# A graph kernel of four layers: TensorE adds up the weighed rows, edge counts are laid out with destinations innermost, and ScalarE copies and turns them one pair later

## The chip, the cores and the metric

The kernel runs on one core of one Trainium2 chip. The metric is the device time of one execution in microseconds (us). The core has TensorE (matmuls, into PSUM), VectorE, ScalarE, GpSimd and SyncE, each with its own in-order queue of instructions. In the profile they are PE (PEld is the loading of the stationary operand), DVE, ACT, POOL and SP; a q behind a name is the queue itself (register, branch and DMA-issuing instructions).

## The reference

A graph of 3125 nodes and 103125 edges, features of 128 floats. Four layers stand one behind the other, each `x = x + layer(relu(layernorm(x)))`. The change touches what two of them and a preparation compute.

```python
# layer 0: three hops of attention over 64 kinds of relation
for _ in range(3):
    h = agg[head]; t = agg[tail]; rel = edge_emb[edge_type]
    att = jnp.sum((h @ q_w) * jnp.tanh(rel * t @ k_w), axis=1)
    w = softmax of att over the edges of each head
    agg = segment_sum(w[:, None] * rel * t, head) / count      # then normalised, added to out
# layer 1: three graph attention layers with 4 heads, layer 2: two graph convolutions
# layer 3: composed attention over 474 kinds
comp = ent_emb[src] + rel_emb[rel_id]
norm = softmax of jnp.sum(comp * ent_emb[dst], axis=-1) over the edges of each dst
out = jnp.tanh(segment_sum(comp * norm[:, None], dst) @ neigh_w)
```

Layers 1 and 2 do not walk over edges. They use a dense matrix with the number of edges between each source and each destination (3200 x 3200), and its logarithm, which a preparation makes once.

## The kernel before

The nodes are sorted by degree and cut into NB = 25 blocks of P = 128, one node on each partition. The edges of a block stand in *bodies*: a body holds S = 8 neighbours for each of the 128 nodes, and a block takes as many bodies as its largest degree needs. All blocks together have 116 bodies. A *half* of a body is H = 4 neighbours.

Every engine runs its own program for a stage, in loops whose counts are read from the plan; semaphores tie the engines together. There is no scheduler: the order on each engine is the order in which the code is written. `stand` is a semaphore wait followed by a count of it, so a wait there shows as "issue" in the trace.

**`count_pairs`** (the preparation) takes the blocks two at a time, 13 *pairs* in all, the last with one block. For a pair VectorE splits the neighbour numbers into a high and a low part (`split`), TensorE turns them, ScalarE copies them out (`splitT`). VectorE makes the one-hot tiles: `hi_hot` of the high part and, in 8 chunks of 16 destinations, `lo_hot` of the low part, two chunks alternating. For a chunk TensorE does 32 matmuls (16 destinations, 2 blocks, contraction over 64 neighbours) into `chunk_ps`, and VectorE adds the chunk into `counts`, which GpSimd has cleared. A pair whose nodes have over 64 neighbours takes more steps of this kind; in this execution each pair takes one. Then TensorE turns the 25 x 2 squares of `counts` (`turn_counts`), ScalarE copies them out in 14 pieces and sends them to memory, and takes the logarithm of `counts` into `logs`; VectorE scales the logs (`tell`), and a DMA that ScalarE issues sends them. `counts`, `logs` and `turned_sb` exist twice.

**`attention_over_relations`** (the relation layers, three hops). GpSimd gathers the rows of a body, eight indirect DMAs (`PairStream.gather_all`); `land` holds two bodies, and `rows_used` gives a half free again. Per body VectorE makes a one-hot of the kinds (`kinds`), multiplies rows and relation vectors (`messages`, one half at the beginning and one at the end of its body), adds the weighed rows of the body before (`add_body`, which calls `Softmax.add`), takes eight dot products (`product`) and does the running softmax (`scores`). TensorE turns the one-hot (`turn_kinds`), turns and projects each half of the messages (`rights`) and makes the relation vectors (`relations`). ScalarE copies between them, takes tanh and the exponentials, and weighs each of the eight rows by its probability (`weigh`, into `weighed`). At the end of a block VectorE divides and stores (`finish_block`).

**`composed_attention`** (the composed layer, one pass over the 116 bodies). Per body TensorE spreads the kinds over all partitions (`widen_kinds`, into `line_ps`), ScalarE copies that line out (`move_line`), VectorE compares it with the kinds (`hots`), and TensorE makes the relation vectors out of 96 bf16 matmuls (`relations`, into `rel_ps`), which VectorE adds to the gathered rows (`compose`). Dot products, softmax, weighing and adding up are as above. VectorE works on body n, composes n+1 and makes one-hots for n+2; TensorE widens n+3.

The rows are added up in `Softmax.add` on VectorE: the 8 x 128 weighed elements of a partition are reduced over the eight (L981), and the running total is scaled (L978) and added to (L984).

## Time and profile before

| | us |
|---|---|
| median of 3 runs (10826.94 to 10835.59) | 10832.68 |
| the profiled execution | 10814.64 |
| its span | 10812.8 |
| pair counts, about 1495 to 2200 of the span | 705 |
| relation layers, three hops, 2310 to 6030 | 3720 |
| graph attention and graph convolution, between | about 3270 |
| composed layer, 9380 to 10760 | 1380 |

The profiled execution's time is the one that its trace adds up to; it lies 18.0 us below the median of the runs. A group of instructions in the profile is named by line, engine, operation, and output and inputs; numbers behind `x` are counts. "Idle before" is time in which the engine stood still ahead of such an instruction, with what ended it behind the arrow.

### The profile page before, as it was taken

The numbers are of one execution on the slowest core, as the hardware profiler recorded it, in microseconds if no ns is written. First come the engines' busy times: TensorE is split into PE (matmuls) and PEld (weight loads), VectorE is DVE, ScalarE is ACT, GpSimd is POOL, SyncE is SP. The second block draws the span as 40 slices with busy tenths as digits, with TensorE's granted clock in tenths as the row PEclk, the third lists the DMA queues.
The fourth block names the chain that finished last, engine by engine and source line by source line (L and its number), as shares of the span: only waits on it lengthen the run. The fifth ranks groups of instructions, "written<-read, shape, count | busy, mean of one in ns | idle before, by whom it ended". The sixth has DMA issues, their size and how long they took to land. (4 is left out here: it accounts for less than half of the span.)

```text
span 10812.8 us, 222859 instructions
## 1 busy us (share of the span) xinstructions
PE 6848.0 (63%) x64938; PEld 5402.2 (50%) x64939; DVE 8324.0 (77%) x22674; ACT 6175.0 (57%) x11492; POOL 6853.0 (63%) x5770
## 2 busy tenths in 40 slices
PE   3984952236666566656666477777777768466665
PEld 2973952235554455545555344444544534366665
DVE  9779778857777677767777699899989970477776
ACT  4224222236666566646666499899979960155554
POOL 0777731057776777767777488878868610466665
PEclk8555556568887788877888799999999989777777
DMA  0111114322222222222222211111111126322212
GB/s 22 57 37 28 60 33 143 129 61 53 53 53 48 49 53 53 53 46 52 53 53 53 38 43 49 50 38 49 46 41 49 49 72 250 74 48 47 46 45 44
DMA packets 415976, 627.20 MB, mean 58 GB/s; under 512 B 273479, under 2 KB 327073, under 8 KB 392169
## 3 DMA queue, kind: packets, MB, share of 16 engines
q0 software_dynamic: 192432, 385.10, 16.3%
q1 hardware_dynamic: 156048, 155.60, 4.6%
q10 hardware_dynamic: 67401, 85.32, 2.2%
q8 instruction: 50, 0.82, 0.0%
q14 instruction: 45, 0.37, 0.0%
HBM read 525.80 MB, written 101.39 MB: 58 GB/s over the span
## 5 line engine op out<-in xcount | busy, mean ns | idle before, releaser
L895 POOL DMA_INDIRECT l_land<-table,l_words x3744 | 3580.1, 956 | 1338.0 <-issue 1153.7
L1674 POOL DMA_INDIRECT ell<-gat_stage_pay,gat_stage_at x816 | 1899.5, 2328 | 248.7 <-issue 248.7
L1365 PE MATMUL left_product_ps<-k_w,messageT 128*128 128x128 f32 x5616 | 1036.5, 341 | 531.6 <-ACT messageT L1400 531.6
L1365 PEld LDWEIGHTS left_product_ps<-k_w,messageT 128*128 128x128 f32 x5616 | 873.4, 237 | 736.4 <-ACT messageT L1400 736.4
L1723 PE MATMUL gat_ps<-gat_probT,h 128*32 128x128 f32 x15000 | 823.7, 292 | 436.2 <-ACT gat_probT L1774 290.3
L2234 PE MATMUL rel_ps<-relation_parts,hot 128*128 128x128 bf16 x11328 | 821.0, 247 | 414.8 <-DVE hot L2333 414.6
L244 POOL DMA_INDIRECT ell<-pay,position x816 | 841.6, 1031 | 290.8 <-issue 281.6
L1359 PE MATMUL left_turned_ps<-ident,message 128*128 128x128 f32 x2808 | 557.7, 333 | 728.2 <-DVE message L1491 728.2
L2234 PEld LDWEIGHTS rel_ps<-relation_parts,hot 128*128 128x128 bf16 x11328 | 800.7, 113 | 436.2 <-DVE hot L2333 436.2
L1416 ACT ACTIVATE weighed<-kept,l_prob 128x128 f32 x2784 | 889.1, 391 | 59.1 <-ACT l_prob L961 59.1
L1714 PE MATMUL gat_ps<-ident,gat_logit 128*128 128x128 f32 x5625 | 824.5, 285 | 44.4 <-ACT gat_logit L1767 43.3
L1851 DVE SCALAR_TENSOR_TENSOR gat_logit<-gat_source_row,gat_own,gat_logit 128x3200 f32<-128x3200 f32 x225 | 797.6, 3545 | 68.3 <-DMA gat_logs<-logs,perm 58.4
L1855 DVE CUSTOM_DVE_ANT_0 gat_logit<-gat_logit,gat_logs 128x3200 f32<-128x3200 f32 x225 | 785.7, 3492 | 27.2 <-issue 2.9
L1359 PEld LDWEIGHTS left_turned_ps<-ident,message 128*128 128x128 f32 x2808 | 384.7, 172 | 830.7 <-DVE message L1491 828.5
L295 PE MATMUL looked_ps<-count,loT_wide 128*128 (+1 forms) x3264 | 755.6, 384 | 48.5 <-issue 45.3
L295 PEld LDWEIGHTS looked_ps<-count,loT_wide 128*128 128x128 f32 x3264 | 744.6, 333 | 57.3 <-issue 54.7
L1351 PE MATMUL rel_ps<-relation_parts,hotT 128*128 128x256 bf16 x4248 | 771.2, 333 | 2.0 <-ACT hotT L1395 2.0
L1412 ACT ACTIVATE right<-left_product_ps 128x512 f32<-128x512 f32 x702 | 418.1, 596 | 602.3 <-DVE l_score L1552 343.3
L1723 PEld LDWEIGHTS gat_ps<-gat_probT,h 128*32 128x32 f32 x15000 | 354.0, 110 | 770.0 <-ACT gat_probT L1774 513.7
L1714 PEld LDWEIGHTS gat_ps<-ident,gat_logit 128*128 128x128 f32 x5625 | 620.7, 142 | 230.7 <-issue 230.7
L1767 ACT ACTIVATE gat_logit<-gat_logit,gat_peak 128x3200 f32<-128x3200 f32 x225 | 667.4, 2966 | 114.9 <-DVE gat_peak L1855 103.3
L981 DVE TENSOR_REDUCE part<-weighed 128x128 f32<-128x1024 f32 x348 | 667.3, 1917 | 27.1
(332 smaller groups left out, 16142.2 us busy)
## 6 DMA issues: line engine op xcount, KB each, us to landing
gcn_edges<-counts SPq DMA_DIRECT2D x50, 1600.0 KB, 7.4
l_land<-table,l_words POOLq DMA_INDIRECT x3744
rows<-low_dram SPq DMA_DIRECT2D x34, 1536.0 KB
counts<-pair_turned_sb ACTq DMA_DIRECT2D x12, 3200.0 KB, 9.4
logs<-pair_logs ACTq DMA_DIRECT2D x12, 3200.0 KB, 18.2
ell<-pay,position POOLq DMA_INDIRECT x816
ell<-gat_stage_pay,gat_stage_at POOLq DMA_INDIRECT x816
l_words<-ell SPq DMA_DIRECT2D x476, 8.0 KB
```

Source lines behind the costliest of these rows:

```text
L244: pool.indirect_dma_start(c.ells[0][:, :], bass.IndirectOffsetOnAxis(ap=position[:, 0, t:t + 1], axis=0), pay[:, t, :], None).then_inc(pla ...
L295: pe.matmul(looked_ps[r % HALVES][:, j, :], loT_wide[:, r % CAST, j, :], count[:, bass.ds(tile + j, 1), :].rearrange("p a n -> p (a n)"), ...
L895: pool.indirect_dma_start(self.land[:, p, s, :], None, table[:, :], bass.IndirectOffsetOnAxis(ap=self.words[:, p, s, 0:1], axis=0)).then_i ...
L1359: mm = pe.transpose(messageT_ps[:, k * H + j, :], message[:, k * H + j, :], c.ident[:, :])
L1365: mm = pe.matmul(right_ps[:, k * H + j, :], messageT[:, k, j, :], k_w[:, :], start=True, stop=True)
L1416: last = nc.scalar.activation(weighed[:, s, :], kept[:, bass.ds(n % 2, 1), s, :].rearrange("p a d -> p (a d)"), ACT.Copy, scale=soft.prob[ ...
L1674: pool.indirect_dma_start(c.ells[1][:, :], bass.IndirectOffsetOnAxis(ap=stage_at[n % 2][:, t:t + 1], axis=0), stage_pay[n % 2][:, t, :], N ...
L1714: mm = pe.transpose(ps[:, q % 4, r * P:(r + 1) * P], logit[t][:, j * P:(j + 1) * P], c.ident[:, :])
L1723: mm = pe.matmul(ps[C * r:C * (r + 1), 4 + t % 2, 0:P], xs[:, 4 * q + r, t * C:(t + 1) * C], probT[q % 4][:, r, :], start=(q == 0), stop=( ...
L1851: V.scalar_tensor_tensor(out=logit[t][:, :], in0=source_row[:, t, :], scalar=own[:, bass.ds(i, 1), t:t + 1].rearrange("p a b -> p (a b)"), ...
L1855: V.tensor_tensor_reduce(logit[t][:, :], logit[t][:, :], logs[k][:, :], op0=ALU.add, op1=ALU.min, scale=-1.0, scalar=3.0e38, accum_out=pea ...
L2234: mm = pe.matmul(rel_ps[:, k * H + s, :], hot[:, k, g, s, :], parts[:, g, t, :], start=(g == 0 and t == 0), stop=(g == PARTS - 1 and t == 2))
```

## The change

Three edits.

In both edge layers (relation layers and composed layer) the eight weighed rows are added by TensorE: eight f32 matmuls with the identity as stationary operand that accumulate in a PSUM tile `sum_ps` (`add_up`). VectorE takes the finished sum in one instruction with the scaling of the total (`Softmax.add_sum`). Two semaphores, `sum_ready` and `sum_used`, pass the tile to and fro.

In `count_pairs` the one-hot tiles and their comparison constants `hi_iota`, `lo_iota` are laid out with the neighbours' or destinations' axis innermost, so that both inputs of the comparison have an innermost step of one element; TensorE then reads columns that lie 128 and 16 elements apart. The first step of a pair is no longer added to cleared counts but copied into them by ScalarE; the clears by GpSimd are gone.

Also in `count_pairs`, the turning, the sending and the logarithm of a pair (`turn_counts` on TensorE, `finish` on ScalarE) stand behind the next pair's counting, and VectorE's `tell` one pair later too.

```diff
+    def add_sum(self, v, total, weighed_sum, sum_ready, n, sum_used):
+        V = self.nc.vector
+        v.wait_ge(self.prob_ready, n)
+        V.tensor_copy(self.top_now[:, :], self.top_new[:, :])
+        V.tensor_reduce(self.part[:, :], self.prob[:, :, :].rearrange("p s h -> p h s"), AX.X, ALU.add)
+        v.drain()
+        V.scalar_tensor_tensor(out=self.denom[:, :], in0=self.denom[:, :], scalar=self.keep[:, 0:1], in1=self.part[:, :],
+                               op0=ALU.mult, op1=ALU.add)
+        v.wait_ge(sum_ready, n)
+        V.scalar_tensor_tensor(out=total[:, :], in0=total[:, :], scalar=self.keep[:, 0:1], in1=weighed_sum[:, :],
+                               op0=ALU.mult, op1=ALU.add).then_inc(sum_used, 1)
...
-        hi_hot = sb("pair_hi_hot", [P, P, NB], BF16)
-        lo_hot = sb("pair_lo_hot", [P, 2, CHUNK, P], BF16)
+        hi_hot = sb("pair_hi_hot", [P, NB, P], BF16)
+        lo_hot = sb("pair_lo_hot", [P, 2, P, CHUNK], BF16)
+        hi_iota, lo_iota = sb("pair_hi_iota", [P, NB, P], BF16), sb("pair_lo_iota", [P, P, CHUNK], BF16)
...
-            @block.gpsimd
-            def _(pool):
-                for p in range(PAIRS):
-                    if p >= 2:
-                        pool.wait_ge(turned, (p - 1) * 2 * TURNS)
-                        pool.wait_ge(logged, p - 1)
-                    nc.gpsimd.memset(counts[p % 2][:, :, :, :], 0.0).then_inc(cleared, 1)
...
-                    pe.wait_ge(summed, p + 1)
+                    many, first = steps(pe, p)
+                    pe.wait_ge(kept, (first + many) * CHUNKS_OF + 2)
...
-                                    mm = pe.matmul(chunk_ps[u % 2][:, b, j * NB:(j + 1) * NB], lo_hot[half, u % 2, j, :],
-                                                   hi_hot[half, u * CHUNK + j, :], start=True, stop=True)
+                                    mm = pe.matmul(chunk_ps[u % 2][:, b, j * NB:(j + 1) * NB], lo_hot[half, u % 2, :, j],
+                                                   hi_hot[half, :, u * CHUNK + j], start=True, stop=True)
...
-                    turn_counts(p, k, parts)
-                pair(0, 0)
+                pair(0)
                 with pe.Fori(0, PAIRS // 2 - 1) as two:
                     for k in range(2):
-                        pair(two * 2 + (k + 1), 1 - k)
-                pair(PAIRS - 2, 1)
-                pair(PAIRS - 1, 0, 1)
+                        pair(two * 2 + (k + 1))
+                        turn_counts(two * 2 + k, k, 2)
+                pair(PAIRS - 2)
+                turn_counts(PAIRS - 3, 0, 2)
+                pair(PAIRS - 1)
+                turn_counts(PAIRS - 2, 1, 2)
+                turn_counts(PAIRS - 1, 0, 1)
...
-                def pair(p, k, earlier, parts=2):
+                def pair(p, k):
                     many, first = steps(act, p)
                     with act.Fori(0, many) as g:
                         n = act.snap(first + g)
                         act.wait_ge(split_turned, n + 1)
                         nc.scalar.copy(splitT[:, :, :], split_ps[:, :, :]).then_inc(split_moved, 1)
+                        with act.If(g < 1):
+                            for u in range(CHUNKS_OF):
+                                act.wait_ge(counted, n * CHUNKS_OF + (u + 1))
+                                nc.scalar.copy(counts[k][:, :, :, u * CHUNK:(u + 1) * CHUNK].rearrange("p h b j -> p b j h"),
+                                               chunk_ps[u % 2][:, :, 0:CHUNK * NB]
+                                               .rearrange("p b (j h) -> p b j h", h=NB)).then_inc(kept, 1)
+                def finish(p, k, earlier, parts=2):
                     act.wait_ge(counts_out[k], earlier * 16 + 16)
...
-                pair(0, 0, 0)
+                pair(0, 0)
+                pair(1, 1)
+                finish(0, 0, 0)
                 with act.Fori(0, PAIRS // 2 - 1) as two:
                     for k in range(2):
-                        pair(two * 2 + (k + 1), 1 - k, two + k)
+                        pair(two * 2 + (k + 2), k)
+                        finish(two * 2 + (k + 1), 1 - k, two + k)
                         tell(two * 2 + k, k)
-                pair(PAIRS - 2, 1, PAIRS // 2 - 1)
+                pair(PAIRS - 1, 0)
+                finish(PAIRS - 2, 1, PAIRS // 2 - 1)
                 tell(PAIRS - 3, 0)
-                pair(PAIRS - 1, 0, PAIRS // 2, 1)
+                finish(PAIRS - 1, 0, PAIRS // 2, 1)
                 tell(PAIRS - 2, 1)
...
-                for k in range(2):
-                    V.memset(logs[k][:, :, :, :], 0.0)
+                V.tensor_copy(hi_iota[:, :, :], spread(c.iota_rb[:, 0:NB], [P, NB, P], 2))
+                V.tensor_copy(lo_iota[:, :, :], spread(c.iota_rb[:, :], [P, P, CHUNK], 2))
...
-                        V.tensor_tensor(hi_hot[:, :, :], spread(c.iota_rb[:, 0:NB], [P, P, NB], 1),
-                                        spread(splitT[:, 1, :], [P, P, NB], 2), ALU.is_equal)
+                        V.tensor_tensor(hi_hot[:, :, :], hi_iota[:, :, :], spread(splitT[:, 1, :], [P, NB, P], 1),
+                                        ALU.is_equal)
                         def hot(u):
-                            V.tensor_tensor(lo_hot[:, u % 2, :, :], spread(c.iota_rb[:, :], [P, CHUNK, P], 1),
-                                            spread(splitT[:, 0, u * CHUNK:(u + 1) * CHUNK], [P, CHUNK, P], 2),
+                            V.tensor_tensor(lo_hot[:, u % 2, :, :], lo_iota[:, :, :],
+                                            spread(splitT[:, 0, u * CHUNK:(u + 1) * CHUNK], [P, P, CHUNK], 1),
                                             ALU.is_equal).then_inc(hot_ready, 1)
                         hot(0)
                         hot(1)
-                        for u in range(CHUNKS_OF):
-                            v.wait_ge(counted, n * CHUNKS_OF + (u + 1))
-                            total = counts[k][:, :, :, u * CHUNK:(u + 1) * CHUNK].rearrange("p h b j -> p b j h")
-                            V.tensor_tensor(total, chunk_ps[u % 2][:, :, 0:CHUNK * NB]
-                                            .rearrange("p b (j h) -> p b j h", h=NB), total, ALU.add).then_inc(kept, 1)
-                            if u + 2 < CHUNKS_OF:
-                                hot(u + 2)
-                        v.drain()
-                    v.sem_inc(summed, 1)
+                        with v.If(g < 1):
+                            for u in range(2, CHUNKS_OF):
+                                v.wait_ge(counted, n * CHUNKS_OF + (u - 1))
+                                hot(u)
+                        with v.If(g > 0):
+                            for u in range(CHUNKS_OF):
+                                v.wait_ge(counted, n * CHUNKS_OF + (u + 1))
+                                total = counts[k][:, :, :, u * CHUNK:(u + 1) * CHUNK].rearrange("p h b j -> p b j h")
+                                V.tensor_tensor(total, chunk_ps[u % 2][:, :, 0:CHUNK * NB]
+                                                .rearrange("p b (j h) -> p b j h", h=NB), total, ALU.add).then_inc(kept, 1)
+                                if u + 2 < CHUNKS_OF:
+                                    hot(u + 2)
...
+                pair(1, 1)
+                with v.Fori(0, PAIRS // 2 - 1) as two:
                     for k in range(2):
-                        pair(two * 2 + (k + 1), 1 - k)
+                        pair(two * 2 + (k + 2), k)
                         tell(two * 2 + k, k)
-                tell(PAIRS - 1, 0)
+                pair(PAIRS - 1, 0)
+                for p in range(PAIRS - 3, PAIRS):
+                    tell(p, p % 2)
...
+                def add_up(w):
+                    pe.wait_ge(sum_used, w + 1)
+                    for k in range(HALVES):
+                        pe.wait_ge(weighed_ready[k], w + 1)
+                    for s in range(S):
+                        mm = pe.matmul(sum_ps[:, :], c.ident[:, :], weighed[:, s, :], start=(s == 0), stop=(s == S - 1))
+                    mm.then_inc(sum_ready, 1)
...
                             rights(n + i + 1, k)
                             relations(m + i + 2, k)
+                        add_up(hop * all_bodies + i)
...
-                    for k in range(HALVES):
-                        v.wait_ge(weighed_ready[k], n)
-                    soft.add(v, weighed, total, part, D)
+                    soft.add_sum(v, total, sum_ps, sum_ready, n, sum_used)
...
+                def add_up(n):
...
                     widen_kinds(i + 3)
+                    add_up(i)
                     for k in range(HALVES):
                         relations(i + 2, k)
...
-                        for k in range(HALVES):
-                            v.wait_ge(weighed_ready[k], n + 1)
-                        soft.add(v, weighed, total, part, D)
+                        soft.add_sum(v, total, sum_ps, sum_ready, n + 1, sum_used)
```

What the program order is at the two places on TensorE and at the one on ScalarE on which the most hangs.

TensorE in the composed layer, the loop over bodies of `composed_attention`, before (`line_ps` is the widening, `rel_ps` the relation vectors):

```order
L2243 UNCONDITIONAL_BRANCH
L2243 ISA
L2223 MATMUL line_ps<-ident_b,kind_b 128x128 x8
L2229 REGISTER_ALU
L2234 MATMUL rel_ps<-relation_parts,hot 128x128 x96
L2243 REGISTER_ALU
L2243 COMPARE_AND_BRANCH
```

The same loop in the change:

```order
L2292 ISA
L2263 MATMUL line_ps<-ident_b,kind_b 128x128 x8
L2280 REGISTER_ALU
L2284 MATMUL l_sum_ps<-weighed,ident 128x128 x8
L2269 REGISTER_ALU
L2274 MATMUL rel_ps<-relation_parts,hot 128x128 x96
L2292 REGISTER_ALU
```

The sum of body i now stands between the widening for body i+3 and the relation vectors of body i+2.

TensorE in the relation layers, the loop over bodies of `attention_over_relations`, in the change (`left_turned_ps` holds the turned messages, `left_product_ps` their projection, each once for a half; before, the same rows stand without the two of the sum):

```order
L1369 MATMUL hotT_ps<-ident_b,hot 128x128 x4
L1386 ISA
L1388 MATMUL left_turned_ps<-ident,message 128x128 x4
L1390 REGISTER_ALU
L1394 MATMUL left_product_ps<-k_w,messageT 128x128 x4
L1376 REGISTER_ALU
L1380 MATMUL rel_ps<-relation_parts,hotT 128x256 x6
L1388 MATMUL left_turned_ps<-ident,message 128x128 x4
L1394 MATMUL left_product_ps<-k_w,messageT 128x128 x4
L1380 MATMUL rel_ps<-relation_parts,hotT 128x256 x6
L1400 ISA
L1404 MATMUL l_sum_ps<-weighed,ident 128x128 x8
```

The sum of body i stands last in its round, behind everything that this round makes for the bodies i+1 and i+2.

ScalarE in `count_pairs`, from the split copy of a pair to the first turned copies, before:

```order
L1131 CAST pair_splitT<-pair_split_ps 128x256
L1128 REGISTER_ALU
L1128 COMPARE_AND_BRANCH
L1132 ISA
L1137 ISA
L1138 COPY pair_turned_sb<-pair_turned_ps 128x512
```

And in the change, the end of the eight chunk copies and what follows them:

```order
L1145 COPY pair_counts<-pair_chunk_ps 128x2x16x25
L1142 UNCONDITIONAL_BRANCH
L1138 REGISTER_ALU
L1138 COMPARE_AND_BRANCH
L1150 ISA
L1155 ISA
L1156 COPY pair_turned_sb<-pair_turned_ps 128x512
```

Eight copies of chunks have come between, and the turned copies behind them are those of the pair before.

## Rows read from the trace of the kernel before

**Rows 1.** By stretch: length, busy PE, PEld, DVE, ACT, POOL; granted clock, DMA.

```profile
1495.00:2200.00 705.00, 181.60 (x3979) 139.98 (x3979) 570.31 (x351) 164.04 (x202) 70.57 (x13) 0.59 0.34 119
2310.00:6030.00 3720.00, 2319.43 (x14222) 1854.47 (x14222) 2778.91 (x12201) 2297.82 (x5958) 2722.26 (x2854) 0.80 0.26 51
9380.00:10760.00 1380.00, 884.10 (x12219) 855.09 (x12217) 1080.12 (x4990) 696.85 (x1630) 894.82 (x930) 0.79 0.24 46
```

**Rows 2.** Who waited for whom, 2320 to 6010: us in total, times, longest.

```profile
POOL l_land L895 <- issue: 866.7, 2777, 5.8
...
DVE hot L1482 <- SPq L864: 394.3, 282, 7.6
```

**Rows 3.** Groups of instructions on GpSimd, 2320 to 6010.

```profile
L895 POOL DMA_INDIRECT l_land<-table,l_words x2796 | 2667.4, 954 | 873.0 <-issue 866.7 <-SPq L864 6.4
```

**Rows 4.** Instructions that read weighed rows: ns min/median/max, first and last start.

```profile
L981 DVE TENSOR_REDUCE l_sum<-weighed x116: 1901/1918/1949, 9397.0 to 10744.8; 128x128 f32<-128x1024 f32 x116
```

**Rows 5.** Timeline of one pair in the counts: start, length in us, instruction.

```profile
1817.84 0.59 ACT L1138 COPY pair_turned_sb<-pair_turned_ps 128x512 f32<-128x512 f32 x1 [35.64 <-PE pair_turned_ps L1088]
...
1827.55 5.63 ACT L1146 ACTIVATE pair_logs<-pair_counts,pair_few 128x6400 f32<-128x6400 f32 x1 [0.60 <-ACT pair_turned_sb L1138]
...
1839.22 0.61 PE L1107 MATMUL pair_chunk_ps<-pair_hi_hot,pair_lo_hot 64*128 64x25 bf16 x32 [10.76 <-DVE pair_lo_hot L1224]
```

**Rows 6.** Instructions of line 1220: ns min/median/max, first and last start.

```profile
L1220 DVE TENSOR_TENSOR pair_hi_hot<-iota_rb,pair_splitT x13: 3491/3493/3493, 1524.0 to 2140.5; 128x3200 bf16<-128x3200 bf16 x13
```

**Rows 7.** Groups of instructions by shape on VectorE, whole span and counts stage.

```profile
L1224 DVE TENSOR_TENSOR pair_lo_hot<-iota_rb,pair_splitT 128x2048 bf16<-128x2048 bf16 x104 | 236.7, 2287 | 0.0
...
L1233 DVE TENSOR_TENSOR pair_counts<-pair_chunk_ps,pair_counts 128x800 f32<-128x800 f32 x104 | 177.0, 1716 | 0.0
...
L1243 DVE SCALAR_TENSOR_TENSOR pair_logs<-pair_logs 128x6400 f32<-128x6400 f32 x13 | 88.7, 6825 | 6.7 <-issue 4.2 <-ACT pair_logs L1146 2.4
...
L675 DVE TENSOR_REDUCE col<-x 128x25 f32<-128x3200 f32 x4 | 14.0, 3488 | 94.9 <-PEq L2422 91.2 <-PEq L599 3.7
...
L1196 DVE MEMSET pair_logs<- 128x6400 f32 x2 | 10.8, 5392 | 3.0 <-issue 3.0
...
L692 DVE TENSOR_SCALAR h<-h 128x3200 f32<-128x3200 f32 x4 | 7.3, 1826 | 0.3
```

**Rows 8.** Timeline of one body in the relation layers.

```profile
4003.61 0.69 DVE L1491 TENSOR_TENSOR message<-l_land,rel_ps 128x512 f32<-128x512 f32 x1
...
4005.93 1.16 PE L1365 MATMUL left_product_ps<-k_w,messageT 128*128 128x128 f32 x8 [0.92 <-ACT messageT L1400]
...
4006.93 0.82 PE L1351 MATMUL rel_ps<-relation_parts,hotT 128*128 128x256 bf16 x6
...
4010.07 0.29 DVE L1552 CUSTOM_DVE_ANT_0 product<-right,left_now 128x128 f32<-128x128 f32 x1
...
4013.00 0.69 DVE L1491 TENSOR_TENSOR message<-l_land,rel_ps 128x512 f32<-128x512 f32 x1
```

**Rows 9.** Timeline of a body, composed layer; relations of a later body.

```profile
10014.51 0.62 PE L2223 MATMUL line_ps<-ident_b,kind_b 128*128 128x128 bf16 x8 [1.94 <-DVE kind_b L2324]
...
10015.38 1.28 ACT L2270 ACT_TABLE_LOAD   x1 [3.94 <-PE line_ps L2223]
...
10018.06 2.45 ACT L2282 ACTIVATE weighed<-kept,l_prob 128x128 f32 x8 [0.17 <-ACT l_prob L961]
...
10019.37 6.91 PE L2234 MATMUL rel_ps<-relation_parts,hot 128*128 128x128 bf16 x96 [4.23 <-DVE hot L2333]
...
10065.08 5.53 PE L2234 MATMUL rel_ps<-relation_parts,hot 128*128 128x128 bf16 x96 [2.04 <-DVE hot L2333]
```

**Rows 10.** Groups of instructions on VectorE, 2320 to 6010, last step of a block.

```profile
L1510 DVE TENSOR_SCALAR res<-total,scale 128x128 f32 x72 | 21.1, 293 | 12.2 <-issue 12.2
```

**Rows 11.** Busy time by stretch as in group 1, during the relations at 10019.37.

```profile
10019.30:10021.00 1.70, 1.63 (x16) 1.64 (x17) 1.70 (x7) 1.70 (x7) 1.40 (x2) 0.50 0.12 28
...
10024.00:10026.30 2.30, 2.27 (x41) 2.10 (x38) 0.76 (x4) 0.00 (x0) 1.82 (x2) 1.00 0.21 57
```

22 lines of the change are left out of this document (16 added, 6 removed).

## The prediction, made before the kernel ran

> **What bounds the kernel now.** I first cut the execution into stages with the windows view. The change touches three of them [rows 1]: the pair counts (705 us), the relation layers with their three hops (3720 us), and the composed layer at the end (1380 us). In each of them VectorE has the largest busy sum, or nearly so, and that sum alone would say: relieve VectorE. The waits say something else.
>
> In the relation layers GpSimd's gathers wait for nothing but their own issue (866.7 us over 2777 gathers, 0.31 us each), while VectorE waits 394.3 us for SyncE's word that rows have landed [rows 2]. A gather takes 0.954 us and with its idle time 3540.4 / 2796 = 1.27 us [rows 3]; eight make a body, and without the long waits 8 x (0.954 + 0.30) = 10.05 us. So GpSimd paces this stage, and VectorE work taken away there buys nothing. What can do harm is a chain that becomes longer than 10.05 us.
>
> In the composed layer the 116 bodies start (10744.8 - 9397.0) / 115 = 11.72 us apart [rows 4], above the 10.05 of the same gathers: here VectorE's chain does set the pace, so a shorter one could win up to 1.67 us a body, 192 us in all.
>
> In the pair counts ScalarE sits idle for 35.64 us before its turned copies [rows 5], and VectorE does everything one after the other: the thirteen first one-hot tiles start (2140.5 - 1524.0) / 12 = 51.4 us apart [rows 6].
>
> **Pair counts: what the change is worth.** A chunk costs VectorE a low one-hot of 2287 ns and an addition of 1716 ns [rows 7]; eight chunks are 32 us of the 51.4. Every pair has one step, so afterwards VectorE adds nothing: ScalarE copies each chunk. The one-hots get an innermost step of one on both 2-byte inputs. No row shows such a two-input operation. Above, its price is today's 2287 ns for 2048 elements; below, the kernel's 3200-element one-input operation that passes two elements a cycle takes 1826 ns [rows 7], 0.57 ns an element, or 1.17 us for 2048. I take the lower one, 1.83 for the high and 1.2 for each low tile, since all operands then lie side by side. The Trainium skill, page "Vector Engine (DVE) Microarchitecture Reference", section 5.1, has a rule for it: two inputs and an output of 2-byte type, all at innermost step one, run two elements a cycle, also where a row is read again and again. By that rule this stage comes to -249 us, by today's row to -120; no row here shows such an operation.
>
> ScalarE's copy is 800 elements from PSUM, written with a jump of 256 elements between neighbours. Below, it costs what a copy of 512 does (0.59 us, [rows 5]) carried to 800, 0.83 us. Above, it costs what VectorE's addition into the same places does, 1.72. VectorE's sum over rows that it reads by jumps takes 1918 ns for 1024 elements [rows 4], 1.87 ns each, against 3488 / 3200 = 1.09 side by side [rows 7]: a jump costs 0.78. 800 x (0.83 + 0.78) + 160 ns gives 1.45 us, which I take. The same page, section 5.2, puts a destination that jumps at every element at 1.71 ns an element for VectorE. By it a copy would take about 1.5 us and the stage would save 4 us less; no row here has ScalarE writing with jumps.
> TensorE's 32 small matmuls of a chunk take 0.61 us [rows 5] and now read both operands with gaps; I allow 1.2 us, hidden beside the copy. Nothing shows it; at over 1.5 us it would be the chunk's pace.
>
> ScalarE now has a pair's whole chain: split copy 0.35; wait for the high tile, the first low tile and the first matmuls, 1.8 + 1.2 + 0.6 and 0.4 of handovers, 4.0; eight copies 11.7; turned copies of the pair before, 1817.84 to 1827.55 with their DMA, 9.7, by [rows 5]; logarithm 5.63 [rows 5]; register loads and gaps, about 2. Sum 33.4 us in place of 51.4. VectorE's own (1.8, 8 x 1.2, 6.8 for the scaling of the logs [rows 7], some 3 for the small steps) is 21 and hidden. Eleven intervals save 11 x 18 = 198 us. The interval between the first two pairs holds no turning: 17.5 in place of 51.4, 34 more. The end gets a second turning and logarithm behind the last chunk (+16) but a shorter last pair (one-hots and additions 3.5 + 8 x 3.9 = 35 before; 3.6 + 11.7 = 15.5 after; -20). At the start VectorE's two clears of the logs, 5.4 us each [rows 7], become two copies of 3200 and 2048 elements, some 4 us in all, and the clears of the counts on GpSimd go, up to 6 more: -13 taken. Together **-249 us**, bounds -120 (VectorE at its old rate, copies hidden) and -310 (copies of 0.83).
>
> **Relation layers.** VectorE loses its sum over eight rows (1.9 us of a body) and waits for TensorE's instead. Read one body [rows 8]. The second message ends at 4004.30 = T. ScalarE turns it over behind its first four weighings; TensorE's products start at 4005.93, its relations end at 4007.75, T + 3.45. Today VectorE starts its dot products at 4010.07 and ends the next second message at 4013.69: a loop of 9.39 us. The new sum stands behind those relations on TensorE's queue. Its price: four f32 products take 1.16 us [rows 8], eight 2.3; bounds 0.62 (eight bf16 matmuls, [rows 9]) and twice 2.3 at half clock. So it ends at T + 5.75, VectorE adds it by T + 6.1, and dot products, scores and message (4010.07 to 4013.69, 3.62) end at T + 9.75. Closing a block lies on this loop too: its last step takes 0.29 us and 0.17 of idle before it [rows 10], three shorter steps and two clears bring it to about 1.4 us, every 348 / 75 = 4.64 bodies, 0.3 a body: **10.05 us, exactly GpSimd's pace**. At equality every delay shows; I put **+70 us** (0.2 a body) on 348 bodies. Nothing is won, since GpSimd's pace stays. The bounds are 0 and, if TensorE falls to its lower clock once a block and 4.1 us of its work in the loop doubles, 4.1 / 4.64 x 348 = +310.
>
> **Composed layer.** Here the place of the new sum on TensorE decides. The program order per body is: widen the kinds of body i+3, sum body i, relations of body i+2, 96 matmuls. ScalarE's order is: copy out the widened line, exponentials of body i, weigh. So the widening waits behind the relations of the body before, the weighing behind the widening, the sum behind the weighing, and the relations behind the sum. All of it is one ring. Its pieces [rows 9]: widening to table load 10014.51 to 10015.38, 0.87; table load and line copy, to the weighing's start at 10018.06, 2.68; weighing 2.45; handover 0.05; sum 2.3; relations 5.53 less 0.1 of overlap, 5.4. Ring: **13.75 us**. Today the ring does not exist: relations start when the one-hots are there, and the weighing of body i delays none of them.
> In the new ring TensorE idles 5.4 us from the widening's end to the sum. In the trace, idle of 4.2 us ahead of the relations has them begin at a granted clock of 0.50 and go on at 1.00 [rows 11], and they take 6.91 us in place of 5.53 [rows 9], 1.4 more. The sum and the relations will pay that: 15.15 us. (15.15 - 11.72) x 115 = **+394 us**. At full clock it would be +233; with 1.4 us more, +555. VectorE's saved 1.92 us [rows 4] only lengthens its wait for the sum. The Trainium skill, page "TensorE: Matmul & The Clock Gate", part "Why this matters for your kernels", advises against idle gaps between bursts of matmuls, since the clock falls in them. It speaks against this ring: by it the body takes 15.15 us, without it 13.75, and the two durations of the relations agree with it.
>
> **Sum.** -249 + 70 + 394 = +215 us. The profiled execution took 10814.6 us (span 10812.8 and 1.8 around it), the median of the three runs is 18 us above it. 10832.7 + 215 = 11048, so **11050 us**. About 0.2% is what a measurement of this kernel can tell from no change.
>
> **The rivals.**
> 1. The composed layer really follows VectorE (*faster*). VectorE's chain without the reduction is at most 11.72 - 1.92 = 9.80 us, so GpSimd's 10.05 would decide: -192 us, relation layers 0, counts -249: 10390 us. For it speaks that today's trace shows VectorE as this stage's pace; against it the program order above. It decides itself at one point: whether the widening starts before the relations of the body before have ended. Chance 0.07.
> 2. A cheap sum (*faster or equal*). Eight matmuls with one and the same stationary operand at about 1.2 us, full clock, copies of 0.83: ring 12.65 (+107), relation layers 0, counts -310, in all about -200: 10630. With only part of it the result is near zero. Chance 0.13.
> 3. The relation layers leave GpSimd's pace, as TensorE drops its clock once a block: +310 in place of +70: 11290. For it: TensorE's work now lies in a loop without slack. Against it: TensorE idles less there than today. Chance 0.12.
> 4. The one-hots stay at one element a cycle, or the gapped operands slow the chunk to over 2 us: counts -120, 11180. Chance 0.08.
> My forecast has 0.60.
>
> **How the numbers follow.** Below 10811 lie rival 1 and most of 2: faster 0.18, same 0.04, slower 0.78. The forecast's own range is 10930 to 11190 (counts by 60, composed layer by 90 either way); taking in rivals 3 and 4 and the upper part of 2, 10790 to 11300.
>
> **What the new profile would show.** Counts: low one-hots of 1.2 us, ScalarE copies of 1.45, first tiles 33 us apart. Relation layers: sums 2.3 us, bodies at 10.0 to 10.4, granted clock nearer 1. Composed layer: bodies 15 us apart, TensorE idle 5 us ahead of the sum and released by the weighing, ScalarE waiting for the widened line, GpSimd waiting for the rows to be used. The prediction is wrong if the bodies there stand 10 to 12 us apart, or if the relation layers grow by more than 200 us.

## The result, and the profile of the changed kernel

The changed kernel takes **11241 us** (median of four runs, 11228 to 11256), the kernel before beside it 10830: a ratio of 1.038, 95% interval [1.0366, 1.0392], slower by 411 us. 11050 was forecast. 11241 lies above the forecast's own range (10930 to 11190) and within the wide one (10790 to 11300), which reaches so far up only because rival 3 (11290) was taken in. The sign and the largest part were right; one term, the relation layers, was far too small.

First the stages, in the windows view of the changed kernel (length of the stretch, busy time of PE, PEld, DVE, ACT and POOL, granted clock, DMA):

```profile
1478.00:1953.00 475.00, 256.42 (x4047) 217.16 (x4046) 264.99 (x272) 326.89 (x309) 0.00 (x0) 0.61 0.51 177
2065.00:6045.00 3980.00, 2856.38 (x19782) 2450.95 (x19782) 2058.97 (x11155) 2287.33 (x5957) 2765.64 (x2851) 0.85 0.25 48
9400.00:11202.00 1802.00, 1156.23 (x14075) 1133.73 (x14073) 849.44 (x4642) 696.49 (x1630) 897.63 (x929) 0.83 0.19 35
```

They answer to [rows 1]. VectorE lost work in all three, 305, 720 and 231 us, and yet two of the three are longer. To measure the edge stages closely, take the first and last start of one instruction that every body has, the update of the running total; before and after (nanoseconds least/median/most, then first and last start):

```profile
L978 DVE TENSOR_TENSOR total<-total,l_keep x348: 278/284/341, 2332.8 to 6008.1; 128x128 f32<-128x128 f32 x174
```

```profile
L973 DVE SCALAR_TENSOR_TENSOR total<-total,l_keep,l_sum_ps x348: 337/347/349, 2084.5 to 6024.5; 128x128 f32<-128x128 f32 x174
...
L973 DVE SCALAR_TENSOR_TENSOR l_total<-l_total,l_keep,l_sum_ps x116: 346/347/350, 9419.0 to 11185.3; 128x128 f32<-128x128 f32 x116
```

The first update comes 2332.8 - 2084.5 = 248 us earlier: the counts. The relation layers grow from 3675.3 to 3940.0, **+265 us**. The composed layer grows from 1347.8 [rows 4] to 1766.3, **+418.5**. Together +435; some 6 us more lie between the stages, and the spans differ by 11254.1 - 10812.8 = 441. The medians differ by 411 only: the profiled execution of before lies 18 us below the median of its runs, the profiled one of the changed kernel 15 above. So the stage figures, read from one execution each, hold some 30 us of scatter in all.

**Pair counts.** The groups of the stage (busy us and mean ns, then idle time before and its releaser):

```profile
L1145 ACT COPY pair_counts<-pair_chunk_ps 128x800 f32<-128x800 f32 x104 | 161.3, 1667 | 56.3 <-PE pair_chunk_ps L1114 56.2
L1114 PE MATMUL pair_chunk_ps<-pair_hi_hot,pair_lo_hot 64*128 64x25 bf16 x3328 | 125.8, 221 | 124.8 <-DVE pair_lo_hot L1245 94.0 <-ACT pair_counts L1145 30.4 <-issue 0.2
L1245 DVE TENSOR_TENSOR pair_lo_hot<-pair_lo_iota,pair_splitT 128x2048 bf16<-128x2048 bf16 x104 | 125.1, 1223 | 24.3 <-PE pair_chunk_ps L1114 24.3
...
L1241 DVE TENSOR_TENSOR pair_hi_hot<-pair_hi_iota,pair_splitT 128x3200 bf16<-128x3200 bf16 x13 | 23.7, 1825 | 136.9 <-ACT pair_splitT L1141 136.9
```

The tile that took 2287 ns [rows 7] takes 1223, the high one 1825 instead of 3493 [rows 6]. ScalarE copies a chunk in 1667 ns, and VectorE waits 136.9 us in all for ScalarE's split copy. ScalarE sets the pace, as forecast.

**Relation layers.** Their waits (us in total, times, longest):

```profile
DVE total L973 <- PE l_sum_ps L1404: 1261.2, 330, 5.7
...
POOL l_land L895 <- issue: 824.3, 2608, 5.7
...
POOL l_land L895 <- DVE message L1531: 242.3, 182, 2.5
...
DVE hot L1522 <- SPq L864: 136.6, 34, 8.2
```

Read against [rows 2] the direction has turned. Before, VectorE waited for rows (394.3 us) and GpSimd for nothing. Now GpSimd waits 242.3 us for VectorE's messages to free its buffer, and VectorE stands still 3.8 us in nearly every body (330 of 348) until TensorE's sum is done. Two bodies one behind the other:

```profile
3001.39 0.69 DVE L1531 TENSOR_TENSOR message<-l_land,rel_ps 128x512 f32<-128x512 f32 x1
...
3005.28 1.95 PE L1404 MATMUL l_sum_ps<-weighed,ident 128*128 128x128 f32 x16
...
3007.26 0.35 DVE L973 SCALAR_TENSOR_TENSOR total<-total,l_keep,l_sum_ps 128x128 f32<-128x128 f32 x1 [2.88 <-PE l_sum_ps L1404]
...
3010.58 0.69 DVE L1531 TENSOR_TENSOR message<-l_land,rel_ps 128x512 f32<-128x512 f32 x1
...
3012.81 1.57 PE L1394 MATMUL left_product_ps<-k_w,messageT 128*128 128x128 f32 x8 [0.83 <-ACT messageT L1439]
...
3014.17 1.49 PE L1380 MATMUL rel_ps<-relation_parts,hotT 128*128 128x256 bf16 x6
...
3015.45 2.60 PE L1404 MATMUL l_sum_ps<-weighed,ident 128*128 128x128 f32 x16
...
3018.09 0.35 DVE L973 SCALAR_TENSOR_TENSOR total<-total,l_keep,l_sum_ps 128x128 f32<-128x128 f32 x1 [2.99 <-PE l_sum_ps L1404]
...
3019.42 0.29 DVE L1548 TENSOR_SCALAR res<-total,scale 128x128 f32 x1 [0.17 <-issue]
```

The first, from message to message, takes 9.19 us. In the second the same three pieces of TensorE's work cost 1.57, 1.49 and 2.60 us, not 1.16, 0.82 and 1.95, and a block closes at its end. The windows view gives the clock of the two sums and of what lies ahead of the second (columns as above):

```profile
3005.40:3007.20 1.80, 1.80 (x20) 1.79 (x19) 0.00 (x0) 0.36 (x1) 1.29 (x2) 1.00 0.15 36
3012.90:3014.30 1.40, 1.40 (x9) 1.34 (x10) 1.04 (x2) 1.40 (x5) 0.94 (x1) 0.68 0.17 47
3014.30:3015.60 1.30, 1.30 (x8) 0.99 (x7) 0.73 (x5) 0.71 (x2) 0.95 (x1) 0.50 0.19 50
3015.60:3018.00 2.40, 2.40 (x19) 2.39 (x18) 0.00 (x0) 0.00 (x0) 1.89 (x2) 0.75 0.21 55
```

**Composed layer.** One turn of the ring in the timeline of the changed kernel:

```profile
10008.32 0.61 PE L2263 MATMUL line_ps<-ident_b,kind_b 128*128 128x128 bf16 x8
...
10009.18 1.28 ACT L2320 ACT_TABLE_LOAD   x1 [9.75 <-PE line_ps L2263]
...
10011.86 2.44 ACT L2332 ACTIVATE weighed<-kept,l_prob 128x128 f32 x8 [0.17 <-ACT l_prob L961]
...
10014.44 3.50 PE L2284 MATMUL l_sum_ps<-weighed,ident 128*128 128x128 f32 x16 [5.52 <-ACT weighed L2332]
...
10017.78 5.52 PE L2274 MATMUL rel_ps<-relation_parts,hot 128*128 128x128 bf16 x96
...
10023.14 0.61 PE L2263 MATMUL line_ps<-ident_b,kind_b 128*128 128x128 bf16 x8
```

Each link releases the next; this turn takes 14.82 us and the mean over 116 bodies is 1766.3 / 115 = 15.36. The sum takes 3.50 us, at a granted clock of 0.53:

```profile
10014.60:10017.70 3.10, 3.10 (x16) 3.10 (x17) 0.00 (x0) 0.72 (x2) 2.31 (x3) 0.53 0.16 45
```

One turn is an example. The waits of the whole stage show the same links in all 116 bodies, and the groups give TensorE's mean (busy us and ns of one record, 16 records a sum and 96 a body's relations):

```profile
ACT L2320 <- PE line_ps L2263: 1061.2, 116, 9.7
...
PE l_sum_ps L2284 <- ACT weighed L2332: 640.1, 116, 5.5
```

```profile
L2274 PE MATMUL rel_ps<-relation_parts,hot 128*128 128x128 bf16 x11223 | 697.3, 227 | 0.0
...
L2284 PE MATMUL l_sum_ps<-weighed,ident 128*128 128x128 f32 x1856 | 420.6, 419 | 640.1 <-ACT weighed L2332 640.1
```

A sum takes 420.6 / 116 = 3.63 us in the mean, so nearly every one of them pays for the lower clock; and the relations never wait for their one-hots, only for the sum ahead of them.

### The profile page after: what moved, and what is told of

It reads as the page before. It is cut to its first block and busy times, and to the rows that moved or that the text cites. A ratio compares the mean times of both kernels' runs of the same rounds, so it can differ in the third digit from the quotient of the medians.

```text
span 11254.1 us, 236447 instructions
## 1 busy us (share of the span) xinstructions
PE 7727.1 (69%) x72362; PEld 6349.4 (56%) x72363; DVE 7061.9 (63%) x21178; ACT 6326.1 (56%) x11596; POOL 6837.0 (61%) x5757
## 5 line engine op out<-in xcount | busy, mean ns | idle before, releaser
L895 POOL DMA_INDIRECT l_land<-table,l_words x3744 | 3629.8, 969 | 1939.6 <-issue 1089.0
L1394 PE MATMUL left_product_ps<-k_w,messageT 128*128 128x128 f32 x5616 | 965.5, 324 | 533.5 <-ACT messageT L1439 532.6
L1394 PEld LDWEIGHTS left_product_ps<-k_w,messageT 128*128 128x128 f32 x5616 | 808.7, 222 | 711.8 <-ACT messageT L1439 710.7
L973 DVE SCALAR_TENSOR_TENSOR total<-total,l_keep,l_sum_ps 128x128 f32<-128x128 f32 x348 | 120.7, 347 | 1261.2 <-PE l_sum_ps L1404 1261.2
L2284 PE MATMUL l_sum_ps<-weighed,ident 128*128 128x128 f32 x1856 | 420.6, 419 | 640.1 <-ACT weighed L2332 640.1
L1404 PEld LDWEIGHTS l_sum_ps<-weighed,ident 128*128 128x128 f32 x5568 | 816.9, 233 | 15.1
L1404 PE MATMUL l_sum_ps<-weighed,ident 128*128 128x128 f32 x5568 | 823.5, 311 | 0.0
L1434 ACT COPY hotT<-hotT_ps 128x512 bf16<-128x512 bf16 x354 | 207.5, 586 | 1042.1 <-PE hotT_ps L1369 1042.1
L1388 PE MATMUL left_turned_ps<-ident,message 128*128 128x128 f32 x2808 | 474.2, 294 | 459.1 <-DVE message L1531 458.9
L2284 PEld LDWEIGHTS l_sum_ps<-weighed,ident 128*128 128x128 f32 x1856 | 395.8, 324 | 656.8 <-issue 656.8
```

What stands on the lines that cost most here:

```text
L895: pool.indirect_dma_start(self.land[:, p, s, :], None, table[:, :], bass.IndirectOffsetOnAxis(ap=self.words[:, p, s, 0:1], axis=0)).then_i ...
L1394: mm = pe.matmul(right_ps[:, k * H + j, :], messageT[:, k, j, :], k_w[:, :], start=True, stop=True)
L1404: mm = pe.matmul(sum_ps[:, :], c.ident[:, :], weighed[:, s, :], start=(s == 0), stop=(s == S - 1))
L2284: mm = pe.matmul(sum_ps[:, :], c.ident[:, :], weighed[:, s, :], start=(s == 0), stop=(s == S - 1))
```

## The experiments

Twelve runs. The first four fell on another chip, on which the kernel before takes 13721 us; their differences are read against that number alone. Two of them were repeated on a chip of 10833 us, and runs 5 to 12 all come from chips on which the kernel before takes 10824 to 10833. The changed kernel itself was measured beside a kernel before of 10830 only, so "less than the changed kernel" compares across chips that agree on the kernel before within 10 us. Three runs (the changed kernel, 6 and 9) have the same code in the relation layers, and their stages are 3940, 3947 and 3955 us: a difference of 15 us between the stages of two runs means nothing. "Relation stage" and "composed stage" are, as above, the time from the first to the last update of the running total.

**1 to 3: one stage changed at a time.** Each keeps one of the three edits and has the code of before in the other two stages.

> Only the pair counts are changed; both edge layers add on VectorE as before. Theory (the stage's gain is what the first sum of the relation layers shows, 249 us earlier, and nothing later takes it back): 10830 - 249 = 10581 us, within 15. Rival (the wider one-hots and copies are partly paid for by a later stage that waits on the logs, so the stage's gain is not the kernel's): over 10620 us.

> Only the relation layers are changed. Theory (TensorE's sum is in VectorE's loop, 0.76 us a body over 348 bodies, as the two traces show between first and last addition): 10830 + 265 = 11095 us, within 25. Rival (the forecast's size, the rest came from elsewhere, such as a collision with the shifted end of the counts): 10830 + 70 = 10900 us.

> Only the composed layer is changed. Theory (the ring over four engines, 15.36 us a body in place of 11.72): 10830 + 418 = 11250 us, within 25. Rival (part of it belongs to the place of the stage in the changed kernel): under 11200 us.

Measured: 13464 (-257, ratio 0.981 [0.980, 0.983]), 14316 (+595, 1.043 [1.042, 1.045]) and 13834 (+113, 1.009 [1.007, 1.010]). The signs agree, the sizes of the second and third do not: on this chip the relation edit costs twice as much, the composed edit a quarter.

**4: the sum between the halves of the relations.**

```diff
                     widen_kinds(i + 3)
-                    add_up(i)
-                    for k in range(HALVES):
-                        relations(i + 2, k)
+                    relations(i + 2, 0)
+                    add_up(i)
+                    relations(i + 2, 1)
```

> The changed kernel, but in the composed layer TensorE adds up body i between the two halves of the relations of body i+2, not ahead of both. Nothing else moves. Theory (the place in TensorE's order made the ring): the relations' first half no longer waits for the weighing, so the ring breaks; VectorE's chain now holds the first half (2.7 us), the sum (2 to 3) and a wait of about 2.4 us behind its last one-hots, so a body takes 12 to 12.5 us: 3.1 x 115 = 330 to 385 us less than the changed kernel, 10870 to 10910. Rival (not the ring but the sum's price itself, 3.5 us of TensorE at its lower clock, costs the time): at most 60 us less, 11180 or more.

Measured 14349 us. Its composed stage was longer than that of run 3 (2077.6 against 1923.9 us). The timeline of run 4 shows how this chip differs:

```profile
13010.06 0.61 PE L2284 MATMUL l_sum_ps<-weighed,ident 128*128 128x128 f32 x4
...
13013.72 0.22 PE L2274 MATMUL rel_ps<-relation_parts,hot 128*128 128x128 bf16 x1 [1.10 <-issue]
...
13014.44 0.27 PE L2274 MATMUL rel_ps<-relation_parts,hot 128*128 128x128 bf16 x2 [0.51 <-issue]
...
13015.39 0.35 DVE L973 SCALAR_TENSOR_TENSOR l_total<-l_total,l_keep,l_sum_ps 128x128 f32<-128x128 f32 x1 [9.37 <-remote]
```

Matmuls of unchanged length (0.1 to 0.2 us) start 0.7 us apart with nothing in the trace that holds them, and VectorE's update stands 4.7 us behind the end of the sum (13010.67). What holds them there the records do not say. The changed kernel did not run on this chip either. Neither theory is decided by such a run.

**5 and 6: counts alone and the sum in the middle, again.**

> The same kernel as in the first experiment, which ran on a chip on which the kernel before took 13721 us in place of 10830; there the counts alone gave 257 us. Theory: the gain does not hang on the chip, 240 to 265 us less than the kernel before beside it (10580 us where that takes 10830). Rival (a fixed share of the stage, larger on a slower chip): less than 230 us on a chip of 10830.

> The same kernel as in the fourth experiment: TensorE adds up body i of the composed layer between the two halves of the relations of body i+2. Where the kernel before takes 10830 us: theory (the ring breaks) 10870 to 10910 us, bodies 12 to 12.5 us apart. Rival from the run on the slow chip, where this order made bodies of 18.07 us against 16.73 (TensorE's second half now stands behind the weighing and the sum, and the widened line of the next body behind that half, so that it is a ring again, through the weighing and half of the relations): 13 to 14.5 us a body, 11000 to 11150 us.

Counts alone: 10606 us (0.979 [0.977, 0.981]), -227. That misses both stated bounds by a little. The trace shows why:

```profile
L991 DVE TENSOR_TENSOR total<-total,l_keep x348: 277/285/338, 2085.8 to 5793.4; 128x128 f32<-128x128 f32 x174
```

The counts gave 2332.8 - 2085.8 = 247 us, but the relation stage, with unchanged code, takes 3707.6 us and not 3675.3. So **32 us of the +265 are not the sum's**. Part of them may be no effect at all: the profiled execution of before lies 18 us below its median. By the medians, 247 - 227 = 20 us are lost behind the counts. The gathers (L895) average 964 ns over the program in place of 956, and the bodies are 0.1 us longer throughout; why, no run tells.

The middle: 11034 us (1.019 [1.017, 1.020]), 207 less than the changed kernel. Its composed stage runs from 9420.0 to 10954.6, 13.34 us a body: the rival's figure (13 to 14.5), not the theory's 12 to 12.5. The ring is not opened by this place: the widening of the next body still stands behind a sum that needs the line of this one; only half of the relations has left the ring.

**7: the update behind the dot products.** In the relation layers only VectorE's order moves. `add_sum` is cut in two: `add_probs` (the wait for the probabilities and the three small instructions behind it) stays, `add_total` (the wait for the sum and the update) and the closing of a block go behind the dot products:

```diff
                             with v.If(body > 0):
-                                add_body(a0 + i)
-                            with v.If(i < 1):
...
+                                soft.add_probs(v, a0 + i)
                             for k in range(HALVES):
...
                                 last.then_inc(right_used[k], 1)
+                            with v.If(body > 0):
+                                soft.add_total(v, total, sum_ps, sum_ready, a0 + i, sum_used)
+                            with v.If(i < 1):
...
```

> The changed kernel, but in the relation layers VectorE adds the finished sum to the running total (and closes a block) behind its dot products, not ahead of them. TensorE's and ScalarE's orders stay. Theory (the sum costs time because VectorE stands still for it ahead of the dot products, 3.8 us a body, and at TensorE's lower clock the loop is over GpSimd's pace): the 2.3 us of dot products now run beside the sum, the loop falls under GpSimd's 10.05 us in most bodies, 200 to 260 us less than the changed kernel. Rival (the granted clock slows all of TensorE's links of the loop, products and relations too, and the sum's place does not matter): at most 100 us less.

Measured 11022 us (1.018 [1.016, 1.020]), 220 less than the changed kernel. The relation stage is exactly as long as with the counts alone (3707.6), and the waits have turned back:

```profile
DVE hot L1531 <- SPq L864: 1144.7, 346, 8.4
POOL l_land L895 <- issue: 869.0, 2774, 5.9
DVE total L982 <- PE l_sum_ps L1413: 120.4, 130, 7.4
```

VectorE waits 3.3 us a body for rows, and GpSimd's wait for messages is gone. The run moves the update and the closing of a block together; how much each of them gives it does not tell.

**8: TensorE kept busy behind the sum.** The extra work in the relation layers writes an unread part of `hotT_ps`:

```diff
+                def warm():
+                    for _ in range(24):
+                        pe.transpose(hotT_ps[:, S - 1, :], c.ident_b[:, :], c.ident_b[:, :])
...
                         add_up(hop * all_bodies + i)
+                        warm()
```

> The changed kernel, but in the relation layers TensorE runs 24 turned copies of a constant behind each sum, into a part of the PSUM that nobody reads (no result hangs on them); about 1.5 to 3 us of work in the idle time ahead of the next body. Theory (the clock's fall to 0.50 in idle time is what makes the loop longer than forecast): granted clock of the stage from 0.85 to over 0.93, 60 to 200 us less than the changed kernel. Rival (the loop is too long at full clock too, or the copies get in the way of the next body's first work): no change or up to 300 us more.

Measured 11164 us (1.030 [1.029, 1.032]), 78 less than the changed kernel:

```profile
2065.00:5950.00 3885.00, 2888.16 (x28134) 2619.82 (x28133) 2044.57 (x11150) 2232.28 (x5955) 2797.30 (x2850) 0.96 0.27 49
```

The clock is 0.96 in place of 0.85, and the stage 3859.3 us in place of 3940.0. TensorE does more and the kernel is faster, so the clock costs at least 81 us. The other 151 remain; how much of them is the price of the 24 transposes themselves can't be told from this run.

**9: the weighing ahead of the line copy.** Composed layer, ScalarE only:

```diff
-                    move_line(i + 3)
                     soft.exponentials(act, i)
                     act.wait_ge(soft.prob_ready, i + 1)
                     for k in range(HALVES):
                         weigh(i, k)
+                    move_line(i + 3)
```

> The changed kernel, but in the composed layer ScalarE weighs the rows of body i first and copies out the widened line of body i+3 behind that. TensorE's and VectorE's orders stay as changed. Theory (the ring runs widening, line copy, weighing, sum, relations, so taking the line copy out of it opens it; what is left starts at the scores: 3.2 us to the end of the weighing, 2.5 the sum, 5.4 the relations, less 0.9 until VectorE needs them, and the clock's share of about 1): bodies 10.5 to 11.7 us apart in place of 15.36, 420 to 560 us less than the changed kernel, 10680 to 10820 us where the kernel before takes 10830. Rival (TensorE's sum ahead of the relations, with its price at the lower clock, is what costs, whatever ScalarE does first): bodies over 13 us, less than 270 us gained.

Measured 10699 us, as the theory has it (0.988 [0.987, 0.990]): this single move takes 542 us off the changed kernel and makes it faster than the kernel before, by 1.2%.

```profile
L973 DVE SCALAR_TENSOR_TENSOR l_total<-l_total,l_keep,l_sum_ps x116: 339/347/350, 9432.2 to 10645.6; 128x128 f32<-128x128 f32 x116
```

And by stretch:

```profile
9400.00:10650.00 1250.00, 974.74 (x14011) 955.00 (x14012) 853.13 (x4644) 694.41 (x1627) 898.60 (x938) 0.93 0.28 51
```

1213.4 / 115 = 10.55 us a body, and a clock of 0.93. TensorE still adds up ahead of the relations, so its place there was not the harm by itself. The move carries two things along:

```profile
L2284 PE MATMUL l_sum_ps<-weighed,ident 128*128 128x128 f32 x1856 | 281.7, 315 | 260.9 <-ACT weighed L2332 260.9
...
L960 ACT ACT_TABLE_LOAD x116 | 148.8, 1283 | 2.1
```

ScalarE's table load (1.28 us a body) stood behind the wait for the line; now it stands ahead of the exponentials and waits for nothing. And the sum falls from 3.63 to 281.7 / 116 = 2.43 us, as TensorE idles less. Load and line copy (2.2 us from the load's start to the exponentials) and the faster sum (1.2) do not make up the 4.8 us a body by themselves: the ring is open, not only shorter.

**10: all later.** Experiments 7 and 9, the sum in the middle (4), and in the composed layer too the update behind the dot products of the next body:

```diff
+                        with v.If(i > 0):
+                            soft.add_total(v, total, sum_ps, sum_ready, n, sum_used)
                         v.drain()
                         soft.scores(v)
...
-                        soft.add_sum(v, total, sum_ps, sum_ready, n + 1, sum_used)
+                        soft.add_probs(v, n + 1)
                         v.drain()
+                    soft.add_total(v, total, sum_ps, sum_ready, first + many, sum_used)
```

> The changed kernel with three edits. Relation layers: the finished sum is added behind the dot products, as in the seventh experiment. Composed layer: ScalarE weighs before it copies the line, TensorE adds up body i between the halves of the relations of body i+2, and VectorE adds the sum to the total behind the dot products of the next body (behind the last body of a block at its end). Theory (with the rings open, VectorE's chain of at most 9.8 us and GpSimd's 10.05 are left): bodies of the composed layer 10.1 to 10.8 us apart, relation layers as with the counts alone, so 10440 to 10530 us where the kernel before takes 10830, and faster than the counts alone (10606). Rival (the waits at the ends of blocks and TensorE's lower clock eat what VectorE saves): 10580 us or more.

Measured **10435 us** (0.964 [0.962, 0.965]). Composed stage 9180.8 to 10367.5, 1186.7 / 115 = 10.32 us a body; relation stage 3703.9. It is the fastest of all, 5 us below the theory's bound and 171 below the counts alone.

**11: the sum ahead of the second half of the relations**, in the relation layers:

```diff
-                        for k in range(HALVES):
-                            rights(n + i + 1, k)
-                            relations(m + i + 2, k)
-                        add_up(hop * all_bodies + i)
+                        rights(n + i + 1, 0)
+                        relations(m + i + 2, 0)
+                        rights(n + i + 1, 1)
+                        add_up(hop * all_bodies + i)
+                        relations(m + i + 2, 1)
```

> The changed kernel, but in the relation layers TensorE adds up body i ahead of the second half of the relations of body i+2, not behind it. VectorE's order stays as changed. Theory (VectorE stands still until the sum's end, and what lies on TensorE ahead of it counts one for one where the loop is over 10.05 us): the sum ends 0.8 us (full clock) to 1.5 us (lower clock) earlier, stage 3940 us down by 120 to 200. Rival (ScalarE's second weighing comes too late for that place, so TensorE waits there and its relations with it): within 60 us of the changed kernel, or slower.

Measured 11003 us (1.017 [1.015, 1.018]), 238 less than the changed kernel, more than the theory's 200:

```profile
L973 DVE SCALAR_TENSOR_TENSOR total<-total,l_keep,l_sum_ps x348: 337/347/349, 2086.0 to 5774.2; 128x128 f32<-128x128 f32 x174
```

And by stretch:

```profile
2065.00:5790.00 3725.00, 2668.81 (x19789) 2282.36 (x19786) 2051.26 (x11155) 2248.23 (x5958) 2739.77 (x2852) 0.92 0.28 51
```

The stage takes 3688.2 us, 252 less than 3940.0, and its clock rose from 0.85 to 0.92 though TensorE does the same work. How much of the gain is the move's own and how much the clock's, this run does not separate.

**12: the two moves alone**, 9 and 11, VectorE's order as in the change.

> The changed kernel with two moves alone: TensorE's sum ahead of the second half of the relations in the relation layers (the eleventh experiment), ScalarE's weighing ahead of the line copy in the composed layer (the ninth). VectorE's order stays as changed. Theory (two separate stages, each repaired by its own move, so the stage lengths of the two runs add): counts -249, relation layers 3688 - 3675 = +13, composed layer 1213 - 1348 = -134, between them +6: 364 us less than the kernel before, 10455 to 10480 us where that takes 10830. Rival (one stage's repair is paid for in the other): over 10520 us.

Measured **10444 us** (0.965 [0.964, 0.966]), 383 less than the kernel before; the relation stage is 3689.1 us, the composed stage 1210.3. Both repairs add, to 11 us beyond the theory's bound; the difference of 9 us to run 10 is smaller than the spread of run 12 by itself (10437 to 10456).

## Why the prediction was right or wrong

**Counts: right.** -249 forecast, -248 by the first update. The tiles take 1.825 and 1.22 us (1.83 and 1.2 taken). ScalarE's copy takes 1.67 (1.45 taken, 1.72 the bound), the eight of a pair 12.4 us (11.7). The first tiles of the first two pairs stand 17.5 us apart (17.5 taken), the others (1888.2 - 1522.8) / 11 = 33.2 (33.4), so the dearer copies were balanced by smaller gaps. The stage begins 1524.0 - 1505.3 = 18.7 us earlier (13 taken), and its end is 4 us worse in place of 4 better; that these two cancel too is luck. TensorE's chunk takes 1.2 us, as allowed. The Trainium skill, page "Vector Engine (DVE) Microarchitecture Reference", section 5.1, has two-byte operands at innermost step one run at two elements a cycle: the trace agrees, with 1223 ns for 2048 elements, 0.60 ns each, in place of 1.12.

**Composed layer: right ring, and a size that two errors helped.** Widening to table load 0.86 us (0.87 taken), table and copy 2.68 (2.68), weighing and handover 2.58 (2.50), sum 3.34 until the relations start, relations 5.36 to the next widening (5.4), TensorE idle for 5.52 ahead of the sum (5.4). At full clock the sum takes 1.95 us, not the 2.3 taken, and in the turn shown 3.50. The lower clock costs the mean sum 3.63 - 1.95 = 1.68 us, and the mean relations 697.3 / 117 - 5.52 = 0.44, together 2.1 us a body. The prediction took 1.4 from [rows 9, 11]. So its price of the clock was too low by 0.7 and its sum too dear by 0.35. +418 measured, +394 forecast. Run 9 shows the ring: opening it at one link gives back 553 of the stage's 1766 us, with TensorE's work unchanged. It also realises rival 1, which failed for the change as written: bodies at 10.55 and, in run 10, 10.32 us.

**Relation layers: the term that failed.** +70 was forecast, +265 measured. The prediction itself had named growth by more than 200 us in this stage as a sign that it is wrong, and that sign came. 32 us appear without any sum (run 5), so the sum costs 232. The failed step is "10.05 us, exactly GpSimd's pace" with 0.2 us a body for equality. Its pieces were not too small: a full-clock body takes 9.19 us and the sum 1.95, less than taken. Two things were wrong. First, the price of the lower clock was put into a rival (chance 0.12, +310) and left out of the sum, though [rows 11] showed it and TensorE's work had just entered the loop. Second, the closing of a block was spread over 4.64 bodies. Sorting the distances between the first dot products of neighbouring bodies by whether a block closes between them (mean us; 72, 74 and 199 distances of each kernel):

| | closing body | the one behind it | all others |
|---|---|---|---|
| before | 11.65 | 9.56 | 9.88 |
| counts alone (5) | 11.78 | 9.69 | 9.95 |
| changed | 11.98 | 11.80 | 10.25 |
| kept busy (8) | 12.10 | 10.15 | 10.40 |
| sum earlier (11) | 11.16 | 10.59 | 9.73 |
| added later (7) | 10.15 | 10.45 | 10.23 |

Before, a closing body overran GpSimd's pace by 1.6 us and the next one made up for a third of it. After the change the body behind a closing is 2.1 us longer than with the counts alone (74 x 2.1 = 156 of the 232 us), the ordinary ones 0.3 (199 x 0.3 = 60) and the closing ones 0.2 (14). Keeping TensorE busy brings that body back to 10.15, from 9.69 with the counts alone. The lower clock itself is not new there. Between the same two dot products, the one behind a closing, the mean granted clock is 0.71 before, 0.70 with the counts alone and 0.72 after the change (0.92 in run 8). The change did not lower the clock; it put TensorE's work where VectorE waits for it, so that the price became visible. What the table does not settle is how much of the 0.3 in ordinary bodies is the clock's: run 8 has them at 10.40, but with its own transposes in the loop. So rival 3's mechanism is the one that happened, most of it once a block, at three quarters of its price.

**Rivals 2 and 4** did not occur. Rival 2 needed a sum of 1.2 us and copies of 0.83; they took 1.95 at the least and 1.67. Rival 4 needed one-hots at the old rate or chunks over 2 us; they took 1.22 us in place of 2.29, and 1.2.

**The total.** 11241 lies within the wide range because the composed layer and the counts came out near their terms and rival 3's price had been taken in. The forecast of 11050 missed nearly half of the change, and the relation term (+265 in place of +70) accounts for it.

## What to carry over

Before work is moved to an idle engine, write down that engine's order and the order of every engine between, and look for a ring: here the harm was not the sum but one ScalarE copy, with its wait and its table load, that stood between a widening and a weighing, and moving it turned +418 us into -134. Where two engines are near the same pace, don't average a rare long body over its neighbours, and price TensorE's part of a new loop at the clock it had after idle time. Ask of each engine whether it ends the longest chain before its lost work is counted as gain: the 720 us taken from VectorE in the relation layers bought at most 20 (3707.6 with VectorE adding, 3688.2 in run 11).

## What the runs showed of the hardware

- Granted clock: from 10008.00 to 10014.40, in which TensorE was busy for 0.93 of 6.40 us, the mean is 0.98; from 10014.60 to 10017.70, in the sum behind it, 0.53. The price of idle time shows in the work that follows it.
- The same clock costs nothing or much: behind the closing of a block 0.71 in the kernel before with bodies of 9.56 us, 0.72 in the changed kernel with bodies of 11.80.
- Eight f32 matmuls with the identity add up eight rows of 128 in 1.95 us at full clock; VectorE's reduction took 1.92. What the exchange changes is which engine waits.
- TensorE's chunk matmuls with gaps in both operands: 221 ns in place of 180, loads 167 in place of 102. ScalarE writing with jumps: 1667 ns for 800 elements.
- One chip ran the same kernel 27% longer with instructions of about the same length (gathers 0.97 us, a sum at full clock 2.00) and idle time between them; an edit that costs 418 us on one chip cost 113 there. An edit that shifts waits must be compared on one chip.
